# State space and MLP of a fused two-layer block on one core: responses raised in the stage before, input norm on two engines, biases shaped within, mean squares per batch

## What is computed

```python
rmsnorm(x, scale) = x * rsqrt(mean(x * x, axis=-1) + 1e-6) * scale
dt   = exp(linspace(log(0.001), log(0.1), 16))
expA = exp(A_ssm); dA = exp(-expA * dt); dB = B_ssm * (1.0 - dA) / expA
step(s, u_t): s = s * dA + u_t[..., None] * dB;  y = einsum('bdn,dn->bd', s, C_ssm)

y = layer norm of x;  u = rmsnorm(y, scale1)      # both from the sum x of the layer before
y = y + (scan of step over u) + u * D_ssm
y = y + gelu(rmsnorm(y, scale2) @ w1 + b1) @ w2 + b2
```

## Time and profile before

| what | value |
|---|---|
| three timed executions | 1437.04, 1439.51, 1439.8 us |
| the profiled execution, its own time | 1435.92 us |
| its span, first to last instruction | 1433.8 us |
| mean granted clock of TensorE | 0.945 |
| busy | PE 1203.1, DVE 913.2, ACT 904.9, POOL 638.9 us |
| stages in the span | attention to 628, swiglu 631 to 793, state_space 793 to 882.5, mlp 882.5 to 1022, experts to the end |

### The profile page before, as it was taken

The page is one execution under the profiler, slowest core; times in us unless marked ns, Lnnn a source line. Parts: engine busy times, 40 slices in busy tenths (PEclk is TensorE's granted clock), DMA queues, the critical chain, the costliest instruction groups (busy, mean ns, idle before and its releaser), DMA issues. The chain is left out here.

```text
span 1433.8 us, 27085 instructions
## 1 busy us (share of the span) xinstructions
PE 1203.1 (84%) x7434; PEld 529.8 (37%) x7434; DVE 913.2 (64%) x2874; ACT 904.9 (63%) x1342; POOL 638.9 (45%) x1047
## 2 busy tenths in 40 slices
PE   4698999999999999948996092999589999999983
PEld 1122222222222222214664092677324333333431
DVE  4477777777777777755996857334355675666542
ACT  2588999999999999933554360333335656566553
POOL 5344556565656664233555300000233555555444
PEclk9999999999999999978999596999889999999997
DMA  4665556555555545149200030000000000000000
GB/s 123 125 118 91 106 103 112 111 104 104 110 107 106 107 100 100 26 95 251 81 0 1 30 118 1 0 0 0 0 1 1 8 16 7 15 15 8 16 16 22
DMA packets 71177, 87.95 MB, mean 61 GB/s; under 512 B 10136, under 2 KB 64958, under 8 KB 65214
## 3 DMA queue, kind: packets, MB, share of 16 engines
q1 hardware_dynamic: 69078, 85.55, 28.6%
q10 hardware_dynamic: 2024, 1.51, 0.5%
HBM read 63.84 MB, written 31.59 MB: 67 GB/s over the span
## 5 line engine op out<-in xcount | busy, mean ns | idle before, releaser
L493 ACT ACTIVATE a_probs<-a_S 128x1024 f32<-128x1024 f32 x512 | 496.6, 1035 | 74.7 <-DVE a_S L635 67.2
L635 DVE TENSOR_TENSOR a_S<-a_S,a_tables 128x256 f32<-128x256 f32 (+1 forms) x512 | 281.3, 561 | 157.5 <-PE a_S L509 154.6
L516 PE MATMUL a_O<-a_probs,a_V 128*32 128x512 f32 x2048 | 275.0, 609 | 2.4 <-ACT a_probs L493 0.6
L509 PE MATMUL a_S<-a_Qs,a_Ks 48*128 48x512 bf16 x1024 | 180.0, 389 | 27.5 <-DMA a_Qs<-a_parts_dram 14.7
L509 PEld LDWEIGHTS a_S<-a_Qs,a_Ks 48*128 48x128 bf16 x1024 | 42.7, 93 | 243.0 <-ACT a_probs L493 194.6
L2005 ACT ACTIVATE e_hid<-e_H 128x512 f32<-128x512 f32 x128 | 69.5, 594 | 80.1 <-PE e_H L2110 80.1
L413 POOL CAST a_parts<-a_whole 128x512 bf16<-128x512 f32 x47 | 29.1, 620 | 157.9 <-DVE a_whole L645 148.8
L1758 ACT ACTIVATE g_hid<-g_H,w_b 128x512 f32<-128x512 f32 x64 | 44.0, 688 | 86.9 <-PE g_H L1779 86.9
L1917 POOL MEMSET e_rT<- 1x512 f32 x1 | 0.5, 518 | 215.8 <-POOLq L1733 215.8
L2108 PE MATMUL e_H<-e_gated,w_We 64*128 64x512 f32 x256 | 74.6, 659 | 12.4 <-DVE e_gated L2208 10.4
L2119 PE MATMUL e_O<-e_hid,w_We 128*64 128x512 f32 x256 | 73.7, 627 | 0.5 <-ACT e_hid L2005 0.5
(11 more groups left out here) (344 smaller groups left out, 2313.7 us busy)
## 6 DMA issues: line engine op xcount, KB each, us to landing
a_parts_dram<-a_parts SPq DMA_DIRECT2D x94, 192.0 KB, 5.6
a_Qs<-a_parts_dram SPq DMA_DIRECT2D x64, 192.0 KB
a_Qs<-a_parts_dram SPq DMA_DIRECT2D x64, 128.0 KB
m_taps_by_step<-h_taps SPq DMA_DIRECT2D x8, 1024.0 KB, 13.5
m_taps<-m_taps_by_step SPq DMA_DIRECT2D x8, 1024.0 KB, 5.2
a_Ks<-a_parts_dram SPq DMA_DIRECT2D x30, 192.0 KB
XY<-L_attn_x SPq DMA_DIRECT2D x16, 256.0 KB, 7.2
a_Qs<-a_parts_dram SPq DMA_DIRECT2D x64, 64.0 KB
```

Source lines behind the costliest of these rows:

```text
L493: act.activation(probs[n % KEPT][:], S[n % RING][:], ACT.Exp).then_inc(exped, 1)
L509: mm = pe.matmul(S[n % RING][:, par, :], Ks[p][rows, pr, kb * P:(kb + 1) * P], Qs[p][Q_OF(kb)][rows, pr, :], start=True, stop=True)
L516: mm = pe.matmul(O[VC * j:VC * (j + 1), :], V[q][:, kb, HG * g + j, :], probs[(2 * m + j // 2) % KEPT][:, j % 2, :], start=(kb == 0), stop ...
L635: v.tensor_tensor(s[:, :, where], s[:, :, where], wide, ALU.mult).then_inc(corrected, 1)
```

## The change

The responses move a stage ahead. `falls` and `rises` now live in `Taps`, which exists from swiglu on. SP loads the rates at the start of swiglu, ahead of all its other DMAs there. ACT makes `rises` at the start of swiglu, ahead of `leading(0, 0)`, with a table load for Exp in front and that for Silu behind; the exponent's step is now counted from 1 (`later`, one more column of the constants), so that no `bias` is needed. At the end of swiglu ACT loads Exp, exps the rates, normalises the third last batch, makes `falls`, and loads Sqrt; DVE's minimum and product come behind the statistics of the second last batch.

In state_space DVE makes `u` of 9 batches and ACT of 7, by `scale` and `bias`; the shift for it is one small DVE instruction more. ACT makes Y of 12 batches and POOL of 4. POOL's large memsets and all its work on Y wait until DVE's part of `u` is done. `shape_biases` comes behind the blocks of sets 0 and 1, ahead of the first sum. The statistics of Y are gone from the stage.

In the MLP each batch's mean squares are made by DVE (4 statistics, 5 small steps) and inverted by POOL: batches 0 and 1 at the start, batch t + 2 in the loop behind the take-out of batch t + 1. The root on ACT and its table load are gone.

```diff
 class Norm:
+    def squares_of(self, v, u, src):
...
+        for c in range(self.core.NT):
+            op = v.bn_stats(st[:, c], src[:, c])
+        op.then_inc(self.steps, 1)
+        v.wait_ge(self.steps, at(1))
+        v.scalar_tensor_tensor(diff, st[..., 1], 2.0, st[..., 1], ALU.mult, ALU.mult)
+        v.scalar_tensor_tensor(square, st[..., 4], 2.0, st[..., 4], ALU.mult, ALU.mult)
+        v.scalar_tensor_tensor(spread, st[..., 2], D * 1e-6, st[..., 5], ALU.add, ALU.add).then_inc(self.steps, 1)
+        v.wait_ge(self.steps, at(2))
+        v.tensor_tensor(square, diff, square, ALU.add).then_inc(self.steps, 1)
+        v.wait_ge(self.steps, at(3))
+        v.scalar_tensor_tensor(self.var4[:, u], spread, 4.0 / D, square, ALU.mult, ALU.add).then_inc(self.steps, 1)
 def swiglu(core, I, W, taps):
         def _(sp):
+            taps.load_rates(sp, I["L1_attn_A_ssm"])
...
-            act.preload_act_table(ACT.Silu)
+            act.preload_act_table(ACT.Exp)
+            taps.rise(act)
             leading(0, 0)
             middle(0, 0)
+            act.preload_act_table(ACT.Silu)
...
             batches(act, body)
+            act.preload_act_table(ACT.Exp)
+            taps.exp_rates(act)
+            for half in range(2):
+                normalise(B - 3, 1, half)
+            taps.fall(act)
             act.preload_act_table(ACT.Sqrt)
-            for b in range(B - 3, B):
+            for b in range(B - 2, B):
...
                 out.moments_of(v, b, None)
+                if b == B - 2:
+                    taps.limit_rates(v)
 class Taps:
+    def rise(self, act):
+        for g in range(self.flt.GROUPS):
+            op = act.activation(self.rises[:, g], self.flt.later, ACT.Exp, scale=self.flt.nrate[:, g:g + 1])
+        op.then_inc(self.rose, 1)
 def state_space(core, I, W, flt, taps):
-    ACT_BATCHES = 11
+    ACT_U, ACT_BATCHES = 7, 12
...
         def _(pool):
+            pool.memset(falls[:, D], 0.0).then_inc(zeroed, 1)
+            pool.wait_ge(dve_ready, U)
             for p in range(2):
                 pool.memset(blocks[p][:], 0.0).then_inc(zeroed, 1)
-            pool.memset(falls[:, D], 0.0).then_inc(zeroed, 1)
...
         def _(act):
+            act.wait_ge(dve_ready, SHIFT)
+            for b in range(B - ACT_U, B):
+                for c in range(NT):
+                    op = act.activation(u[:, b, c], X[:, b, c], ACT.Identity, bias=ushift[:, b, c:c + 1],
+                                        scale=core.urstd[:, b, c:c + 1])
...
         def _(pe):
-            pe.wait_ge(act_ready, FALLS)
-            pe.wait_ge(zeroed, 3)
+            pe.wait_ge(zeroed, 1)
             pe.wait_ge(dve_ready, U)
+            pe.wait_ge(act_ready, ACT_UPPER)
...
             for s in range(2):
                 lay_blocks(s)
+            v.wait_ge(states, tick.start + tick.n)
+            W.shape_biases(nc, ctx, v, faded[:].rearrange("p g b -> p (g b)"))
             v.wait_ge(act_ready, ACT_A)
...
             v.wait_ge(bank_free, SETS * (SET // PER))
-            for b in range(B):
-                for c in range(NT):
-                    v.bn_stats(core.yst[:, b + 1, c], Y[:, b + 1, c])
 def mlp(core, I, W):
+        @block.gpsimd
+        def _(pool):
+            power.constant(pool, init, 0)
+            power.invert(pool, 0, rstd)
+            power.invert(pool, 1, rstd)
+            def body(t, p, i):
+                power.invert(pool, t + 2, rstd)
...
             def rms_norm(b, last=False):
+                v.wait_ge(power.inverted, b * Norm.INVERT + Norm.INVERT)
...
+            power.squares_of(v, 0, Y[:, 1])
+            v.wait_ge(*W.mlp)
+            v.tensor_scalar(w1[:], w1[:], s2[:], None, ALU.mult).then_inc(scaled, 1)
+            power.squares_of(v, 1, Y[:, 2])
             rms_norm(0)
             take_T(0, 0)
-            W.shape_biases(nc, ctx, v)
...
                 take_T(t + 1, 1 - p)
+                if not isinstance(t, int):
+                    power.squares_of(v, t + 2, Y[:, t + 3])
```

More of the change, by code:

```diff
@@ L1569, in state_space @@
         sem = lambda n: core.sem("m_" + n)
-        u, shift = sb("u", [P, B, NT, D]), sb("shift", [P, B, NT])
-        falls = sb("falls", [P, D + 1, N])
-        rises = sb("rises", [P, GROUPS, P])
-        rates = rises[:].rearrange("p g t -> p (g t)")[:, 0:D * N]
+        u = sb("u", [P, B, NT, D])
+        shift, ushift = core.in_mean, core.in_rstd
+        falls, rises = taps.falls, taps.rises
         state, faded = sb("state", [P, GROUPS, B * CARRY]), sb("faded", [P, GROUPS, B])
```

118 lines of the change are left out of this document (57 added, 61 removed).

## The result

The changed kernel took 1401.16 us (median of 4 runs, 1399.44 to 1404.04) against 1439.65 us (1437.04 to 1440.86) before: ratio 0.9739, 95% interval 0.9719 to 0.976. Forecast were 1404.1 us and 1400 to 1412. The kernel of before was run again beside each set of experiments; its medians there were 1437.39 to 1439.34 us.

A forecast was written before the change was run, and what follows sets the result against it. PE was taken to set the time within the scan and MLP loop, with gains only where it stands still. Terms -17.2 - 12.5 - 6.2 + 0.5 = -35.4 us from the median 1439.51 gave 1404.1 us, range 1400 to 1412.

The forecast's parts named there:

- Start of state_space: Ahead of the scan's first matmul: PE starts at 805.0 instead of 822.18, ACT's `u` being last; -17.2 us.
- Within the scan: In state_space: delayed carry steps and the biases leave the first sum 3 us ahead of set 2; 0 us.
- Statistics and start of the MLP: Two terms: DVE's 64 statistics behind the scan go, -12.5 us; last sum to first MLP product shortens, -6.2 us.
- MLP loop: In each MLP batch: POOL's inverse comes half an us late, but within the cover, so 0 us.
- So there is 1.1 us of cover: In the MLP's loop: delay that POOL's chain can take before PE waits; beyond it each us costs 15.
- The first rival: In the MLP's loop: POOL's inversions late, half an us beyond the cover costing 7.5 us, 1411.6 us; chance 0.08.
- The clock part of that rival: In the MLP's loop: late `yn` makes PE pause and drop to 1.2 GHz, up to 115 us more; chance 0.02.
- The MLP's first products: PE's eight first MLP products, 5.19 us before: clock recovery left undecided, a possible gain of 1 to 2 us not counted.
- End of swiglu: At swiglu's end: POOL's sum held up by DVE's product, inversions behind it 0.5 us later; +0.5 us, bounds 0 and 1.2.
- Start of swiglu: At swiglu's start: 32 exps at 0.293 us on idle ACT, hidden with 1.7 us to spare; 0, bounds 0 and +2.6.
- The second rival: At swiglu's start or end: cover thinner, exps at 0.43 or code late, +2.6 to 5 us; chance 0.12.
- The sum: Whole kernel: -17.2 - 12.5 - 6.2 + 0.5 = -35.4 us, taken from the median 1439.51 us.

The follow-up runs named there:

- a1: Changed kernel, but POOL no longer waits until DVE's part of `u` is done: 1407.66 us, ratio 0.979.
- a7: Changed kernel with 15 of 16 batches' inputs normalised on ACT and 1 on POOL, instead of 12 and 4: 1402.75 us, ratio 0.9743.
- a4: Changed kernel with the shaping of the biases back in the MLP, behind the first transposes: 1408.17 us, ratio 0.9791.
- a5: Changed kernel with the 64 statistics back behind the scan and one chain for all batches at the MLP's start: 1415.34 us, ratio 0.9837.
- a8: Changed kernel with two idle power steps more in POOL's inversion of each batch in the MLP: 1433.08 us, ratio 0.997.
- a9: Changed kernel with one small multiplication more in POOL's inversion of each batch in the MLP: 1398.53 us, ratio 0.9722.
- b2: Changed kernel with 15 batches on ACT, the rates' exps at swiglu's start, and idle PE matmuls ahead of scan and MLP: 1400.47 us, ratio 0.9742.
- a0: The changed kernel measured once more, nothing edited: 1400.66 us, ratio 0.9745.
- a3: Changed kernel with the 32 exps of `rises` at swiglu's start given a `bias` operand again: 1405.43 us, ratio 0.978.

## Why the prediction was right, and where it was not

- **Start of state_space**: -17.2 forecast, 29.22 to 11.96 is -17.3. ACT was last, at 0.389 us a piece (0.386 taken). a1 shows that the pace of DVE hangs on POOL's silence: 0.92 us a piece beside POOL, 0.26 as soon as it is done.
- **Within the scan**: 0 forecast, +0.8 to +0.9 measured, a missed cost. The term that was mis-sized is the delay of DVE's carry steps, put at one POOL operation, 1.04 us: three of the four steps took 1.48 to 1.59 us instead of 0.88, 2 us in all. The step also looked only at set 2, for which 3 us were free, and never asked when PE wants set 0's blocks, which was at 837.26 - 17.2 = 820.1. Its 821.2 is the end of the blocks of both sets; set 0's would have been done 1.4 us earlier, so with 1.04 us PE would have had them in time, and with 2 us it waits. a7 and a1 take the wait away. Other kernels with the same code show +0.4 to +1.0. The biases themselves cost nothing, as said.
- **Statistics and start of the MLP**: -12.5 - 6.2 = -18.7 forecast, 26.50 to 7.90 is -18.6. a4 and a5 give it back in two parts, cut otherwise than the prediction's two terms: 7.9 us for the biases and 10.75 for the statistics less what POOL's inversion costs; together 18.6.
- **MLP loop**: 0 forecast, and the period stayed at 7.66 us, but with far less to spare than said. "So there is 1.1 us of cover" is the step that failed: the cover is 0.25 us by a8 and by a9. To add DVE's slack and PE's along one chain was sound; the terms of the chain were too short. From the end of the take-out to the inverse it had 1.6 + 0.18 + 2.52 = 4.3 us; in the changed kernel's loop it is 0.95 for the statistics, 1.03 for the five small steps (0.71 at the MLP's start), 0.27 until POOL begins and 2.66 for the inversion, 4.9 us, and 0.2 more pass until DVE begins `yn`, for which nothing was counted. Behind `yn` the transposes hold the take-out back for 0.75 us (a8, a9), not 0.6. That makes the ring 7.41 us where the prediction's own terms give 6.5. The first rival was thus nearer than 0.08 said, and that the 0 came out true is in part luck: a9's step of 0.38 us was enough to lengthen each batch. By a8's prices, x at the start and 14 (x - 0.25) in the loop, a delay of x = 2.6 us takes back the 35.4 us, and not 3.5; a8's 2.37 took 32 of the 38. The clock part of that rival didn't come: PE's products ran at 3.60 us in a8 too.
- **The MLP's first products**: nothing was counted. They took 5.1 to 6.4 us against 5.19, so up to 1.2 us lost, of the size named and of the other sign. The rows behind 863.79 show a granted clock of 0.50 (1.2 GHz) until 869. b2 shows what was there to be had: 2.9 us.
- **End of swiglu**: +0.5 forecast, 0.0 in a0 and +1.45 in the first profile, the difference being PE's clock. POOL's sum was held up by DVE's product as feared (1.96 us instead of 1.27), but its inversion had 0.58 us of slack behind it. The Trainium skill (ScalarE: Activation LUTs, section "What ACT_TABLE_LOAD costs") puts a drain of about 1.38 us to each load, by which ACT would be late by 1.1 us; here the trace disagrees: in a0 the load begins 0.01 us behind the activation ahead of it (774.85), takes 1.28, and the exp begins 0.02 us behind it (776.15).
- **Start of swiglu**: 0 forecast and -0.3 to -0.5 measured, at 0.296 us an exp (0.293 taken). The second rival needed the slower form, which a3 makes: +1.5 us and not +2.6, since that form runs at 0.385 and not at 0.43.
- **The sum**: -35.4 us. The touched places (swiglu's table load to the MLP's end) took 403.3 us before and 370.1 after, -33.2 us in the first profile, and -35.3 in a0. The two profiled totals differ by 33.3 us, the medians by 38.5. The 3 us by which the median came out under the forecast lie in no touched place: the profiled execution of before was 3.7 us under its median, that of the changed kernel 1.5 us above. Carrying the difference of one execution over to a median was good to some 3 to 5 us, more than any error of a term.

## What to carry to other kernels

When work of a batch is split over engines in a loop, write down the ring (who starts whom, over the batch's edge), take each of its terms, the hand-overs too, from rows of the same kind of place, and compare its length with the period; here five terms that were 0.1 to 0.4 us too short each left 0.25 us of a cover of 1.1. Keep GpSimd silent while VectorE runs the instructions that PE waits for, and give the work to whoever stands still then. Judge an edit of a few us by the stretch that it touches, since the total carries several us of other things; how well a stretch repeats differs, 0.02 us for the way to the scan here and 0.6 for the scan.
